# A fused conditional layer and top-1 expert FFN: x gathered by itself, b2 spread by TensorE, the condition sum as one contraction, low halves of x's second half on GpSimd

## The chip, the core and the metric

The kernel runs on one core of a Trainium2 chip. The core has TensorE (PE, matrix products into PSUM), VectorE (DVE), ScalarE (ACT), GpSimd (POOL) and SyncE (SP), which issues DMAs; ScalarE and GpSimd issue DMAs too. The metric is the device time of one execution in microseconds (us), lower is better.

## The reference

2048 tokens of 256 values pass a linear layer whose weights depend on the batch entry, then a feed-forward network with one expert of eight per token, and are added to the input.

```python
# x (2, 1024, 256), cond_8 (2, 8), weight (8, 256, 256), mask (256, 256), bias (256)
masked_w = weight * mask[None, :, :]
w_bot = jnp.einsum('bg,got->bot', y, masked_w)
xf = jnp.einsum('bnt,bot->bno', x, w_bot) + bias        # the conditioned rows
logits = xf @ gate_w.T + gate_b
top1 = jnp.argmax(logits, axis=-1)
for e in range(8):
    h = jax.nn.relu(xf @ w1[e].T + b1[e])               # 256 -> 1024
    y = h @ w2[e].T + b2[e]                             # 1024 -> 256
    out = out + jnp.where((top1 == e)[:, None], y, 0)
return x + out
```

## The kernel before

Products that carry the result are made of float16 pairs: a value is split into a high half (a rounded copy by ScalarE) and a low half (the remainder, by VectorE), and TensorE adds high x high, high x low and low x high. The tokens are sorted by expert into slot tiles of 128 tokens of one expert; this input has 21 such tiles, the first five of expert 0.

**Head.** SP loads y, the eight condition weights in four DMAs of 0.5 MB, the mask, and the transposed x in two halves of 1 MB, then expert 0's four weight chunks and b2, copied to every partition (1 MB). VectorE forms the weighted sum for batch entry 0 in eight steps (lines 603 and 605), TensorE the one for entry 1 with diagonal matrices of y that ScalarE writes (lines 459, 864). Both are multiplied by the mask. `fold_gate` (line 812) multiplies the gate into the sum, `gate_logits` (line 841) gives the logits from x in float32, `turn_w` (line 804) transposes the sum, `w_t_out` and `w_t_low` (lines 469, 621) split it. `x_high(q)` and `x_low(q)` (lines 465, 616) split quarter q of x. `rows(t)` (line 828) makes the conditioned rows of 128 tokens in six matmuls, ScalarE writes them to `xf` (line 503), and SP stores them in five DMAs to the left half of `both_rows` in DRAM (line 347). ScalarE has x copied to its right half by two DMAs of 1 MB (`x_store`, line 485).

**Routing.** VectorE takes the argmax in five steps (lines 661 to 665); TensorE waits for it (`oh_ready`) after three row groups and ranks the tokens; VectorE computes each token's slot, TensorE turns that into `tok_of_slot` (line 894). Each VectorE step waits for the one before (`then`). VectorE then derives a plan for each tile (lines 707 to 726): its expert, and `goal`, how many of the 14 late w2 chunks are split by that tile. It is three per two tiles (`usual_goal`) or two per expert begun, whichever is more.

**Tile loop.** GpSimd gathers the rows of a tile from `both_rows`, 2 KB per token (line 423), eight tiles ahead (`RING`), and scatters the results (line 430). For tile i TensorE transposes the gathered rows of tile i + 1 (`turn_x`, line 916), does layer 1 of tile i (line 928) and layer 2 of tile i - 1 (line 944). ScalarE, in this order: `x_hi(i + 1)`, `w1_high(i + 1)` when its expert is new (two chunks, line 523), the w2 chunks due (`split_chunks`, `high_late`, line 513), `seed_h(i + 1)` (b1 into PSUM, line 543), `h_hi(i)` (line 560), `seed_y(i)` (b2 into PSUM, line 552). VectorE does the low halves in the same order and adds x to the result (`y_out`, line 768). Each engine runs its own list in order.

**Weights.** Each expert has four chunks of 0.5 MB, in the order w1, w2, w1, w2. SP issues them, counts them in `landed` once they have arrived (`confirm`, line 341) and keeps three in flight from expert 2 on. `high_late(m)` waits until 2(m + 2) + 2 chunks have landed. Expert 1's chunks follow the last row store; the last two wait for gathers 0 and 1, expert 2's first for gather 2.

TensorE also does products of ones that nobody reads (`keep_clock_up`, line 855): ten at the start and 24 after the routing. Six more prime the PSUM banks (line 902).

## Time and profile before

| | us |
|---|---|
| median of 3 runs | 173.21 |
| lowest, highest | 172.95, 176.34 |
| the profiled execution | 172.72 |
| its span, first to last instruction | 170.9 |
| TensorE busy | 156.6 |
| VectorE busy | 112.2 |
| ScalarE busy | 106.7 |
| GpSimd busy | 60.1 |

All times in the rows below are of the profiled execution and count from the start of its span; 1.8 us of the time lie outside the span. Busy times are sums over stages with different limits, and TensorE's include the unread products.

### The profile page before, as it was taken

What the parts mean: (1) busy time and instruction counts of PE and PEld (TensorE: products, weight loads), DVE (VectorE), ACT (ScalarE), POOL (GpSimd) and SP (SyncE); (2) the same over time, 40 slices, a digit from 0 to 9 for tenths busy, and PEclk for the clock granted to TensorE, in tenths of its full rate; (3) what the DMA queues carried; (4) which work ended last, traced back from release to release, by engine and by line L of the source; (5) the groups of instructions that cost most, each with busy time, mean ns of one, the idle gap of its engine ahead of it and who ended that gap; (6) DMA issues with size and microseconds to landing.
All of it is one profiled execution on the core that took longest, in us unless ns stands there. A gap on an engine that the chain in (4) does not pass through costs nothing.

```text
span 170.9 us, 6123 instructions
## 1 busy us (share of the span) xinstructions
PE 156.6 (92%) x1807; PEld 132.9 (78%) x1807; DVE 112.2 (66%) x217; ACT 106.7 (62%) x192; POOL 60.1 (35%) x59
## 2 busy tenths in 40 slices
PE   5999899994899999799799799999999999999970
PEld 2347588742689999799789799999999998898850
DVE  0396899980957768999999996345872552258300
ACT  3505988103295988999999968466754465566300
POOL 8300000037830255065666466442464201220222
PEclk9999999999999999999999999999999999999998
DMA  3999999949849788999999912322301101000100
GB/s 71 345 410 411 409 400 385 368 110 332 257 135 314 224 300 303 339 314 295 323 300 344 315 63 84 98 84 65 94 33 42 45 23 35 31 10 31 36 19 19
DMA packets 13797, 33.40 MB, mean 195 GB/s; under 512 B 2619, under 2 KB 6843, under 8 KB 13632
## 3 DMA queue, kind: packets, MB, share of 16 engines
q1 hardware_dynamic: 8288, 24.39, 40.8%
q0 software_dynamic: 2688, 6.30, 11.8%
q10 hardware_dynamic: 2784, 2.26, 4.0%
q8 instruction: 17, 0.28, 0.7%
q14 instruction: 20, 0.16, 0.3%
HBM read 30.06 MB, written 6.95 MB: 217 GB/s over the span
## 4 chain that ended last, share of the span: by engine, by line
PE 57%; DMA 18%; issue 9%; ACT 7%; ACTq 3%; DVE 1%; POOL 1%; SPq 1%; DVEq 1%; POOLq 0%
PE psum L944 21%; PE psum L928 19%; DMA wsp<-w_all 14%; PE psum L828 6%; PE psum L864 4%; PE psum L855 3%; DMA rows_in<-both_rows,tok_of_slot 2%; DMA both_rows<-stage 2%; ACT wsp L513 2%; ACT psum L543 2%; PE psum L916 1%; PE psum L841 1%; PE psum L812 1%; ACTq L284 1%; ACT stage L523 1%
## 5 line engine op out<-in xcount | busy, mean ns | idle before, releaser
L944 PE MATMUL psum<-wsp,hT 128*128 x504 | 58.5, 273 | 1.5 <-issue 1.1
L944 PEld LDWEIGHTS psum<-wsp,hT 128*128 128x128 f16 x504 | 48.1, 98 | 7.8 <-issue 2.6
L763 DVE SCALAR_TENSOR_TENSOR hT<-psum,hT 128x512 f16<-128x512 f32 x42 | 27.3, 687 | 22.6 <-ACT hT L560 22.2
L430 POOL DMA_INDIRECT out<-rows_in,tok_of_slot x17 | 19.9, 1170 | 58.7 <-DVE rows_in L768 58.7
L423 POOL DMA_INDIRECT rows_in<-both_rows,tok_of_slot x17 | 23.4, 1376 | 36.1 <-issue 36.1
L543 ACT ACTIVATE psum<-b_col 128x1024 f32 x21 | 21.5, 1022 | 21.3 <-issue 21.3
L928 PE MATMUL psum<-xs,w1s_own 128*128 128x128 f16 x528 | 31.6, 219 | 0.8 <-issue 0.8
L928 PEld LDWEIGHTS psum<-xs,w1s_own 128*128 128x128 f16 x528 | 30.1, 98 | 2.2 <-issue 1.8
L928 PE MATMUL psum<-xs,stage 128*128 128x128 f16 x480 | 28.4, 219 | 2.8 <-ACT psum L543 2.8
L928 PEld LDWEIGHTS psum<-xs,stage 128*128 128x128 f16 x480 | 27.3, 98 | 3.9 <-issue 2.2
L560 ACT ACTIVATE hT<-psum 128x512 f16<-128x512 f32 x42 | 22.9, 588 | 4.2 <-PE psum L928 2.4
L641 DVE SCALAR_TENSOR_TENSOR wsp<-wsp (+1 forms) x16 | 19.2, 1223 | 6.0 <-ACT wsp L513 4.0
L535 ACT ACTIVATE xs<-psum,bias_col 128x128 f16<-128x128 f32 x42 | 13.2, 369 | 12.0 <-PE psum L916 8.7
L754 DVE SCALAR_TENSOR_TENSOR xs<-psum,bias_col,xs 128x128 f16<-128x128 f32 x42 | 12.7, 346 | 7.4 <-issue 4.7
L513 ACT ACTIVATE wsp<-wsp x14 | 14.9, 1064 | 3.4 <-SPq L341 2.5
L650 DVE SCALAR_TENSOR_TENSOR w1s_own<-wsp,w1s_own 128x1024 f16<-128x1024 f16 (+1 forms) x10 | 11.9, 1223 | 2.3 <-ACT w1s_own L523 2.0
L855 PE MATMUL psum<-ones_h 128*128 128x512 bf16 x38 | 10.8, 445 | 1.9 <-POOL ones L398 1.9
L828 PE MATMUL psum<-stage,wsp 128*128 128x256 f16 x96 | 10.8, 273 | 0.7 <-issue 0.7
L768 DVE SCALAR_TENSOR_TENSOR rows_in<-psum,rows_in 128x256 f32<-128x256 f32 x17 | 7.1, 418 | 5.8 <-PE psum L944 5.8
L828 PEld LDWEIGHTS psum<-stage,wsp 128*128 128x128 f16 x96 | 9.3, 98 | 1.9 <-issue 0.9
L855 PEld LDWEIGHTS psum<-ones_h 128*128 128x128 bf16 x38 | 4.1, 110 | 7.2 <-issue 2.2
L430 POOL DMA_INDIRECT out<-stage,tok_of_slot x4 | 5.4, 1353 | 12.0 <-DVE stage L768 12.0
(113 smaller groups left out, 138.9 us busy)
## 6 DMA issues: line engine op xcount, KB each, us to landing
wsp<-w_all SPq DMA_DIRECT2D x32, 512.0 KB
wsp<-cond_w SPq DMA_DIRECT2D x4, 512.0 KB, 6.8
wsp<-x_t SPq DMA_DIRECT2D x2, 1024.0 KB, 10.7
both_rows<-x_rows ACTq DMA_DIRECT2D x2, 1024.0 KB, 14.8
b_all<-b SPq DMA_DIRECT2D x1, 1024.0 KB, 18.2
both_rows<-stage SPq DMA_DIRECT2D x1, 768.0 KB, 7.3
both_rows<-stage SPq DMA_DIRECT2D x1, 512.0 KB, 6.1
both_rows<-stage SPq DMA_DIRECT2D x1, 384.0 KB, 4.9
```

What stands on the lines that cost most here:

```text
L423: g.indirect_dma_start(slot(i % RING), None, both_rows, token(i), bounds_check=TOK - 1, oob_is_err=False).then_inc(x_in[i % RING], 16)
L430: g.indirect_dma_start(out, token(i), res(i % RING), None, bounds_check=TOK - 1, oob_is_err=False).then_inc(stored[i % RING], 16)
L513: a.mul(hi_of(m + EARLY), raw_w2(m + EARLY), WSCALE).then_inc(hi_ready, 1)
L535: last = a.activation(xs[:, b, 0, k * P:(k + 1) * P], ps_xT[b][:, k * P:(k + 1) * P], ACT.Identity, bias=bias_col[:, k:k + 1])
L543: a.mul(psum[:, 1 + 2 * b:3 + 2 * b, :].rearrange("p q (c n) -> p (q c) n", n=P), b1_col[:, bass.ds(e * KH, KH)].unsqueeze(2).to_broadcast ...
L560: a.activation(hT[:, b, 0, q * HALF:(q + 1) * HALF], ps_h[b][q], ACT.Relu).then_inc(hhi_ready, 1)
L641: v.scalar_tensor_tensor(lo_of(n), raw_w2(n), WSCALE, hi_of(n), ALU.mult, ALU.subtract).then_inc(lo_late, 1)
L763: v.scalar_tensor_tensor(hT[:, b, 1, q * HALF:(q + 1) * HALF], ps_h[b][q], 0.0, hT[:, b, 0, q * HALF:(q + 1) * HALF], ALU.max, ALU.subtrac ...
L828: last = t_.matmul(ps_rows[t % 4], x16[:, xp, k, t * P:(t + 1) * P], w_t[:, b, wp, k * D:(k + 1) * D], start=(k + xp + wp == 0), stop=(k = ...
L855: t_.matmul(psum[:, 6, :], ones_h[:, :], ones_h[:, :].unsqueeze(1).to_broadcast([P, 4, P]), start=True, stop=True)
L928: last = t_.matmul(o, w1s[b][:, w:w + P], xs[:, b, xp, k * P:(k + 1) * P], start=False, stop=(c % 4 == 3 and k == KD - 1 and wp == 1), ski ...
L944: last = t_.matmul(ps_y[b], hT[:, b, hp, c * P:(c + 1) * P], w, start=False, stop=(c == KH - 1 and w is low), skip_group_check=True)
```

## The change

- **Condition sum.** The weights come in four DMAs of 0.5 MB laid out with (16 output rows, 8 conditions) on the 128 partitions. One matrix `y_block`, built by ScalarE from `own_o` (GpSimd) and y, contracts the eight conditions for both batch entries at once on TensorE: 4 x 4 matmuls of 256 columns, each on a strip of 32 columns. The result holds both entries, 16 output rows each, on a strip. VectorE multiplies it by the mask, which is loaded doubled (0.5 MB), in four parts; `fold_gate` and `turn_w` go over the four parts in turn, ahead of the logits. The gate bias is formed in the same layout (16 matmuls of one column). Four unread products stand after each of the first three parts.
- **Small inputs** come in one DMA from ScalarE's queue; the mask and b2 follow there.
- **b2** is loaded once (8 KB) and spread by TensorE (ones times b2, four matmuls of 512 columns in float32) and four ScalarE copies. Two banks are primed in place of six, 16 unread products follow in place of 24.
- **Gathers.** `x_store` goes. A tile's conditioned rows are gathered from `xf_rows` (1 KB per token), and its rows of x by a gather of its own from the input, which `y_out` alone waits for.
- **SP's order.** Expert 0's chunks wait for the first half of x. Two of expert 1's chunks are issued ahead of the row stores and two right behind them. Expert 2's first loads wait for gather 0 in place of gather 2.
- **Low halves.** GpSimd forms `x_low(2)` and `x_low(3)`; VectorE's `w_t_low(1)` and first `w1_low` move; ScalarE does both `w_t_out` ahead of `x_high(0)`, and the first `early_w1_high` after row group 1. The argmax is waited for after four row groups.
- **Goals.** A tile's goal is two w2 chunks for each earlier tile that kept its expert, or two per expert begun, whichever is more. `split_chunks` moves to the end of ScalarE's and VectorE's work on a tile.

```diff
...
-        RANKS_AFTER = 3
-        HIGH_AFTER = (2, 6, 10)
+        RANKS_AFTER = 4
+        HIGH_AFTER = (1, 4, 7, 10)
...
-            sp.dma_start(mask, cond_mask).then_inc(ld_mask, 16)
+            for n in range(OQ):
+                sp.dma_start(condw[:, n, :], cond_w[n]).then_inc(ld_cw[n], 16)
...
+                sp.dma_start(xf_rows[t * P:end * P, :].rearrange("(t p) d -> p t d", p=P),
                              xf[:, t:end, :]).then_inc(rows_stored[n], 16)
...
+            sp.wait_ge(ld_x[0], 16)
             for q in range(CPE):
                 load_chunk(0, q)
-            sp.dma_start(b2_all[:, :, :], b2.partition_broadcast(P)).then_inc(ld_b2, 16)
             for q in range(CPE):
                 confirm(q, 1)
+            for q in range(CPL):
+                load_chunk(1, q)
             for n in range(len(STORES)):
                 store_rows(n)
+            for q in range(CPL, CPE):
+                load_chunk(1, q)
             sp.wait_ge(rows_ps, TT)
-            for n in range(len(STORES)):
-                sp.wait_ge(rows_stored[n], 16)
-            load_chunk(1, 0)
-            load_chunk(1, 1)
             sp.wait_ge(x_in[0], 16)
-            load_chunk(1, 2)
-            sp.wait_ge(x_in[1], 16)
-            load_chunk(1, 3)
             for q in range(CPE):
                 confirm(q, LOADED // CPE)
...
-            sp.wait_ge(x_in[2], 16)
-            sp.wait_ge(wbot0_ready, 1)
-            sp.wait_ge(wbot1_ready, 1)
+            sp.wait_ge(wbot_ready, OQ)
             for q in range(IN_FLIGHT):
                 load_chunk(LOADED // CPE, q)
...
+            for q in (2, 3):
+                pool.wait_ge(x16_hi_ready, q + 1)
+                g.tensor_tensor(x16[:, 1, :, quarter(q)], xT[:, :, quarter(q)], x16[:, 0, :, quarter(q)],
+                                ALU.subtract).then_inc(x16_lo_ready[q], 1)
...
             def gather(i):
                 if i >= RING:
+                    pool.wait_ge(xT_ps, i - RING + 1)
+                g.indirect_dma_start(xg(i % RING), None, xf_rows, token(i),
+                                     bounds_check=TOK - 1, oob_is_err=False).then_inc(x_in[i % RING], 16)
+            def gather_res(i):
+                if i >= RING:
                     pool.wait_ge(stored[i % RING], 16 * (i // RING))
-                g.indirect_dma_start(slot(i % RING), None, both_rows, token(i),
-                                     bounds_check=TOK - 1, oob_is_err=False).then_inc(x_in[i % RING], 16)
+                g.indirect_dma_start(res(i % RING), None, x_rows, token(i),
+                                     bounds_check=TOK - 1, oob_is_err=False).then_inc(res_in[i % RING], 16)
...
-            pool.wait_ge(x_stored, 32)
-            for i in range(RING):
+            for i in range(FIRST):
                 gather(i)
+            for i in range(FIRST, RING):
+                gather_res(i - FIRST)
+                gather(i)
+            for i in range(RING - FIRST, RING):
+                gather_res(i)
...
+                    if_used(pool, used, i + RING - 1, lambda: gather_res(i + RING - 1))
                     if_used(pool, used, i + RING - 1, lambda: gather(i + RING - 1))
...
+            act.dma_start(small[:, :], small_t).then_inc(ld_small, 16)
+            act.dma_start(b2_all[0:1, :, :].rearrange("p e n -> p (e n)"), b2.rearrange("e n -> (e n)").unsqueeze(0)).then_inc(ld_b2, 16)
+            act.dma_start(mask, cond_mask.rearrange("p (a n) -> p a n", a=OQ)).then_inc(ld_mask, 16)
...
+            act.wait_ge(ld_small, 16)
+            act.wait_ge(own_o_ready, 1)
+            for b in range(B):
+                a.mul(y_block[:, b * ON:(b + 1) * ON], own_o[:, :], y_col[:, b:b + 1]).then_inc(y_block_ready, 1)
...
-                act.wait_ge(wT_ps, b + 1)
-                a.mul(w_t[:, b, 0, :], ps_wT[b], WSCALE).then_inc(wT_ready, 1)
+                act.wait_ge(wT_ps, 1)
+                a.mul(w_t[:, b, 0, :].rearrange("p (k a n) -> p k a n", k=KD, n=ON), ps_wT_of[b], WSCALE).then_inc(wT_ready, 1)
...
-            x_store(0)
+            w_t_out(0)
+            w_t_out(1)
             x_high(0)
             x_high(1)
-            x_store(1)
             act.wait_ge(logit_bias_ready, 1)
             act.wait_ge(logits_t_ps, 1)
             a.activation(logits_t[:, 0:XC], ps_logits_t[0], ACT.Identity, bias=logit_bias[:, 0:1]).then_inc(logits_t_ready, 1)
             x_high(2)
-            w_t_out(0)
             x_high(3)
-            w_t_out(1)
-            early_w1_high(0)
...
-                if t == HIGH_AFTER[0]:
-                    early_w1_high(1)
+                if t in HIGH_AFTER[:CPL]:
+                    early_w1_high(HIGH_AFTER.index(t))
                 elif t in HIGH_AFTER:
-                    early_w2_high(HIGH_AFTER.index(t) - 1)
+                    early_w2_high(HIGH_AFTER.index(t) - CPL)
...
+            b2_flat = b2_all[:, :, :].rearrange("p e n -> p (e n)").rearrange("p (a n) -> p a n", n=512)
+            act.wait_ge(b2_ps, 1)
+            for n in range(E * D // 512):
+                a.copy(b2_flat[:, n, :], psum[:, 1 + n, :]).then_inc(b2_ready, 1)
...
                 if_used(act, used, i + 1, lambda: w1_high(i + 1, 1 - b, plan.next_expert, plan.next_expert - plan.expert))
-                if_used(act, used, i + 1, lambda: split_chunks(act, high_late, plan.goal, plan.next_goal))
                 next_plan = following_plan(act, i, plan)
                 if_used(act, used, i + 1, lambda: seed_h(i + 1, 1 - b, plan.next_expert))
                 if_used(act, used, i, lambda: h_hi(i, b))
                 if_used(act, used, i, lambda: seed_y(i, b, plan.expert))
+                if_used(act, used, i + 1, lambda: split_chunks(act, high_late, plan.goal, plan.next_goal))
...
-            v.tensor_tensor(wbot[:, 1, :, :].rearrange("p k n -> p (k n)"), ps_wbot1, mask, ALU.mult).then_inc(wbot1_ready, 1)
+            for n in range(OQ):
+                dve.wait_ge(cond_ps, n + 1)
+                v.tensor_tensor(wbot[:, n, :], ps_cond[n], mask[:, n, :], ALU.mult).then_inc(wbot_ready, 1)
...
+                dve.wait_ge(wT_ready, B)
+                v.scalar_tensor_tensor(w_t[:, b, 1, :].rearrange("p (k a n) -> p k a n", k=KD, n=ON), ps_wT_of[b], WSCALE,
+                                       w_t[:, b, 0, :].rearrange("p (k a n) -> p k a n", k=KD, n=ON),
                                        ALU.mult, ALU.subtract).then_inc(wT_lo_ready, 1)
...
+            dve.wait_ge(gate_ps, 1)
+            v.tensor_copy(gate_w[:, :, :, :].rearrange("p k b n -> p k (b n)"), ps_gate_both).then_inc(gate_w_ready, 1)
+            w_t_low(0)
+            w_t_low(1)
             x_low(0)
             dve.wait_ge(logit_bias_ready, 1)
             dve.wait_ge(logits_t_ps, 2)
             v.tensor_scalar(logits_t[:, XC:2 * XC], ps_logits_t[1], logit_bias[:, 0:1], None,
                             ALU.add).then_inc(logits_t_ready, 1)
             x_low(1)
-            w_t_low(0)
...
-            x_low(2)
-            w_t_low(1)
...
-            x_low(3)
...
-            w1_low(0, 0, 0, 0)
...
-            then(v.tensor_scalar(goal_f[:, 0, :], tile_e[:, :], float(CPL), None, ALU.mult))
-            then(v.tensor_tensor(goal_f[:, 0, :], goal_f[:, 0, :], usual_goal[:, :], ALU.max))
-            then(v.tensor_scalar(goal_f[:, 1, :], goal_f[:, 0, :], float(W2_CHUNKS - EARLY), 0.0, ALU.min, ALU.max))
+            then(v.tensor_tensor(stays[:, 2:NT], tile_e[:, 2:NT], tile_e[:, 1:NT - 1], ALU.is_equal))
+            then(v.tensor_tensor_scan(goal_f[:, 0, :], ones[:, 0:NT], stays[:, :], 0.0, ALU.mult, ALU.add))
+            then(v.tensor_tensor(goal_f[:, 0, :], goal_f[:, 0, :], tile_e[:, :], ALU.max))
+            then(v.tensor_scalar(goal_f[:, 1, :], goal_f[:, 0, :], float(CPL), float(W2_CHUNKS - EARLY), ALU.mult, ALU.min))
...
+            w1_low(0, 0, 0, 0)
...
+                dve.wait_ge(res_in[r], 16 * (i // RING + 1))
...
                 if_used(dve, used, i + 1, lambda: w1_new(i + 1, 1 - b, plan.next_expert, plan.next_expert - plan.expert, plan.next_same))
-                if_used(dve, used, i + 1, lambda: split_chunks(dve, low_late, plan.goal, plan.next_goal))
                 next_plan = following_plan(dve, i, plan)
                 if_used(dve, used, i, lambda: h_lo(i, b, plan.goal))
+                if_used(dve, used, i + 1, lambda: split_chunks(dve, low_late, plan.goal, plan.next_goal))
...
+            def fold_gate(n):
+                for k in range(KD):
+                    last = t_.matmul(ps_gate[k], wbot[:, n, k * P:(k + 1) * P], gate_x[:, n, :],
+                                     start=(n == 0), stop=(n == OQ - 1))
+                if n == OQ - 1:
+                    last.then_inc(gate_ps, 1)
+            def turn_w(n):
+                for k in range(KD):
+                    last = t_.transpose(ps_wT[k][:, n * P:(n + 1) * P], wbot[:, n, k * P:(k + 1) * P], ident[:, :])
+                if n == OQ - 1:
+                    last.then_inc(wT_ps, 1)
...
+            pe.wait_ge(y_block_ready, B)
+            for n in range(OQ):
+                pe.wait_ge(ld_cw[n], 16)
+                for j in range(CG):
+                    last = t_.matmul(ps_cond[n][j * EP:(j + 1) * EP, :], y_block[:, :], condw[:, n, j * D:(j + 1) * D],
+                                     start=True, stop=True)
+                last.then_inc(cond_ps, 1)
+                if n < OQ - 1:
+                    keep_clock_up(CLOCK_GAP)
+                if n == 0:
+                    for q in range(OQ):
+                        for j in range(CG):
+                            last = t_.matmul(ps_gate_bias[j * EP:(j + 1) * EP, :], gate_x[:, q, 0:EP], bias_x[:, q:q + 1],
+                                             start=(q == 0), stop=(q == OQ - 1))
+                    last.then_inc(gate_bias_ps, 1)
+            pe.wait_ge(logit_bias_ready, 1)
+            for n in range(OQ):
+                pe.wait_ge(wbot_ready, n + 1)
+                fold_gate(n)
+                turn_w(n)
             gate_logits(0)
             gate_logits(1)
-            turn_w(0)
+            rows(0)
             pe.wait_ge(logits_t_ready, 2)
             turn_logits(0)
             turn_logits(1).then_inc(logits_ps, 1)
-            turn_w(1)
-            for t in range(RANKS_AFTER):
+            for t in range(1, RANKS_AFTER):
                 rows(t)
...
                     t_.matmul(psum[:, 3, 0:D], ones_h[:, :], ones_h[:, :].unsqueeze(1).to_broadcast([P, 2, P]),
                               start=True, stop=True)
             pe.wait_ge(rows_ready, TT)
-            for bank in range(1, 7):
+            pe.wait_ge(ld_b2, 16)
+            pe.wait_ge(consts, N_CONST)
+            for n in range(E * D // 512):
+                last = t_.matmul(psum[:, 1 + n, :], ones[0:1, :], b2_all[0:1, 2 * n:2 * n + 2, :].rearrange("p e n -> p (e n)"),
+                                 start=True, stop=True)
+            last.then_inc(b2_ps, 1)
+            for bank in range(5, 7):
                 last = t_.matmul(psum[:, bank, :], ones_h[:, :], ones_h[:, :].unsqueeze(1).to_broadcast([P, 4, P]),
                                  start=True, stop=True)
...
-            keep_clock_up(24)
+            keep_clock_up(16, 6)
             pe.wait_ge(experts_known, 1)
...
```

## Rows read from the trace of the kernel before

**Rows 1.** The page's chain that ended last, by line.

```profile
PE psum L944 21%; PE psum L928 19%; DMA wsp<-w_all 14%; PE psum L828 6%; PE psum L864 4%; PE psum L855 3%; DMA rows_in<-both_rows,tok_of_slot 2%; DMA both_rows<-stage 2%; ACT wsp L513 2%; ACT psum L543 2%; PE psum L916 1%; PE psum L841 1%; PE psum L812 1%; ACTq L284 1%; ACT stage L523 1%
```

**Rows 2.** The chain in order of time: start us, us, what.

```profile
22.34 8.53 PE psum L828 x78
31.30 4.14 DMA both_rows<-stage
...
49.93 4.73 DMA wsp<-w_all
...
62.83 5.49 DMA wsp<-w_all
...
100.88 2.68 PE psum L928 x48
103.55 2.62 PE psum L944 x24
```

**Rows 3.** Busy time by window: engines, then granted clock, DMA share, GB/s.

```profile
6.00:14.00 8.00, 7.97 (x24) 3.67 (x23) 6.85 (x10) 0.73 (x4) 0.00 (x0) 1.00 1.03 407
60.00:98.00 38.00, 35.33 (x474) 32.79 (x472) 35.20 (x52) 36.20 (x58) 20.20 (x12) 1.00 0.94 315
```

**Rows 4.** Timeline, TensorE, first layer of tiles 0, 5 and 9.

```profile
43.61 2.62 PE L928 MATMUL psum<-xs,w1s_own 128*128 128x128 f16 x40 [0.33 <-issue]
...
70.80 2.84 PE L928 MATMUL psum<-xs,stage 128*128 128x128 f16 x48 [0.89 <-ACT psum L543]
...
95.19 2.84 PE L928 MATMUL psum<-xs,stage 128*128 128x128 f16 x48 [0.85 <-ACT psum L543]
```

**Rows 5.** Timeline, ScalarE, splits of weights.

```profile
65.17 2.00 ACT L523 ACTIVATE stage<-wsp 128x1024 f16 x2
...
68.68 1.06 ACT L513 ACTIVATE wsp<-wsp  x1 [0.56 <-SPq L341]
```

**Rows 6.** Line 327, the condition weights' DMAs: issues, and us to landing.

```profile
L327 SPq DMA_DIRECT2D wsp<-cond_w x4: 408/432/723, 1.3 to 2.7; - x4
...
DMA to landing us min/median/max: 4.9/6.8/8.1
```

**Rows 7.** Timeline, TensorE, head.

```profile
1.88 4.42 PE L855 MATMUL psum<-ones_h 128*128 128x512 bf16 x10 [1.88 <-POOL ones L398]
...
6.33 7.23 PE L864 MATMUL psum<-wsp,hT 128*128 128x512 f32 x16
...
13.76 1.95 PE L812 MATMUL psum<-gate,stage 128*128 128x32 f32 x16
...
15.64 2.01 PE L841 MATMUL psum<-wsp,gate_w 128*32 128x256 f32 x32
```

**Rows 8.** Timeline, ScalarE and VectorE, head.

```profile
14.74 1.04 ACT L465 CAST wsp<-wsp 128x1024 f16<-128x1024 f32 x1 [0.48 <-issue]
...
18.27 0.60 ACT L469 ACTIVATE stage<-psum 128x512 f16<-128x512 f32 x1
...
19.92 0.28 DVE L661 TENSOR_REDUCE best<-psum 128x16 f32<-128x128 f32 x1
...
21.21 0.71 DVE L665 TENSOR_TENSOR oh<-e_less,first 128x128 bf16<-128x128 f32 x1
```

**Rows 9.** Timeline, TensorE, from the routing to the first transpose.

```profile
34.20 5.34 PE L855 MATMUL psum<-ones_h 128*128 128x512 bf16 x24
41.80 0.41 PE L916 MATMUL psum<-ident,rows_in 128*128 128x128 f32 x2 [2.26 <-DMA rows_in<-both_rows,tok_of_slot]
```

**Rows 10.** Timeline, GpSimd, and one VectorE instruction beside it.

```profile
2.93 2.65 POOL L414 MEMSET rows_in<- 128x3072 f32 x1
...
36.59 1.18 POOL L423 DMA_INDIRECT rows_in<-both_rows,tok_of_slot  x1 [31.01 <-issue]
...
76.03 1.22 DVE L641 SCALAR_TENSOR_TENSOR wsp<-wsp  x1
76.16 2.01 POOL L423 DMA_INDIRECT rows_in<-both_rows,tok_of_slot  x1 [0.30 <-issue]
```

182 lines of the change are left out of this document (75 added, 107 removed).

## The prediction

> **What bounds the kernel now.** I read the page's chain by line first, then the chain in order of time, then the windows, then the timelines of the stretches that change. The chain is 40% TensorE's two expert layers (lines 944 and 928) and 14% a wait for expert weights [rows 1]. In order of time it has three parts [rows 2]. The head, up to the first expert tile at 43.6 us [rows 4], runs through the condition sum, the logits, the 16 matmul groups of the conditioned rows (line 828, last piece ending 30.87), the last store of those rows (4.14 us) and the gather. Then comes a stretch bound by weights: the chain's loads land at 54.7 and 68.3. From 95.19 TensorE alone sets the pace, 2.68 + 2.62 and 0.22 for two transposes, 5.52 us per tile.
>
> DMA moves 407 GB/s in the head and 315 at a share of 0.94 between 60 and 98 [rows 3]. From the first tile (43.61) to the tenth (95.19) TensorE takes 51.6 us, where tile 0 (4.06 before the next starts) and eight at 5.52 would be 48.2 [rows 4]. The missing 3.4 us are stalls of about 1 us ahead of tiles 5, 7 and 9. The first follows ScalarE's split that could start only at 68.68, when expert 3's last chunk had landed [rows 2, 5]; the other two come of ScalarE, which in each of these tiles splits 1.5 w2 chunks beside 2 w1 chunks, at 1.0 to 1.06 us each [rows 5]. The later 71.5 us are TensorE's and the change doesn't touch them.
>
> **Condition sum and gate.** Removed: 8 VectorE steps, 16 matmul records of 512 columns (lines 603 to 607, 864), ScalarE's 8 y_diag. Added on TensorE, which is free of the warm-up at 6.3 [rows 7]: 16 matmuls of 256 columns on 32-column strips, 32 records. Line 841 does 32 such records in 2.01, so 2.0 in all. 12 clock dummies at 0.22 (5.34/24, rows 9): 2.7. The gate bias in 32 one-column records: between nothing and the 0.125 of line 812's records; nearest in weights are line 841's at 0.063, and one column streams less, so I take 0.04: 1.3. Sum 12.3. The last cond_w chunk landed 8.1 after its issue at 2.7, at 10.8 [rows 6]. The doubled mask puts 0.26 MB more beside it (0.6 us at 407 GB/s, rows 3) and the small loads, merged into one, give some back: about 11.3, so TensorE decides. Fold and turn are 24 records at 0.125 [rows 7]: 3.0, so the transposed weights stand at 15.3 and gate_w at 15.6. The gate logits still end with x, whose bytes ahead change by +0.26 MB: 17.5, against 17.65 [rows 7]. So the faster contraction buys nothing: x sets this point.
>
> **The order behind it.** ScalarE now does both w_t halves (0.60 each) ahead of x_high, so that x_high(0), 1.04, begins at 16.6 and not 14.74 [rows 8]. VectorE: w_t low twice (I take 0.7 each, 512 elements from PSUM beside ScalarE's 0.60) to 18.0, x_low(0) (1.22, as line 641 on 1024 elements, rows 10) to 19.2, logits_t to 19.7, x_low(1) to 20.9; argmax then takes the 2.0 between 19.92 and 21.92 [rows 8] and ends at 22.9, a microsecond later than before. TensorE puts row groups 0 to 3 ahead of it, idles 0.3, and does the other 12 at 0.67 (8.53/13 with its gaps): end 31.35, against 30.87. x_low(2) and (3), and the w1 low half, leave VectorE's chain behind the argmax, 3 times 1.2. That chain then ends about with the row groups, so routing is not later than before.
>
> **GpSimd's two subtractions.** GpSimd has no such row. From below, its 3072-element memset took 2.65 [rows 10], so 1024 elements take 0.9; from above, if each of the three operands went at that rate, 2.6. They may start at about 20 and are wanted at 26.3 (group 8) and 29 (group 12): hidden either way for TensorE. What they cost VectorE is the first rival.
>
> **Stores, gathers, b2.** x_store (2.1 MB) and the broadcast b2 (1.05 MB) leave the head's DMA, which was saturated until the last store; 1.05 MB of expert 1 moves in at about 22. The last store should take 3.2 in place of 4.14 [rows 2], bounds 2.8 and 4.1. So gather 0 is issued at 36.1 (36.59 before, rows 10), is half as large and meets no 1 MB load issued just ahead of it: 3.5 in place of 5.2, landed at 39.6 against 41.8 [rows 9]. It is what SP waits for before expert 2's first load: 39.6 in place of 49.93 [rows 2], the largest shift of the change. GpSimd issues 16 gathers in place of 8, at 1.3 each, until 57, then three DMAs per tile (up to 1.7 + 2.0 + 2.0 + 0.9 = 6.6 us beside VectorE's splits, rows 10) against 5.5. It falls behind by some 10 us over tiles 0 to 9, covered by the seven tiles (38 us) that a gather runs ahead. Without the cover each tile would cost 1.1.
> TensorE pays for b2: 4 matmuls of 512 columns, two f32 records each, as line 864's 16 between 6.33 and 13.56, of which those without a wait took 0.43 [rows 7]: 3.4; four priming matmuls and 8 dummies fewer, 2.7 less. From 31.35: token matmuls 2.2, b2 3.4, priming 0.4, 16 dummies 3.6, register loads 0.3: first transpose at 41.2 against 41.80 [rows 9], so tile 0 at 43.0 against 43.61. ScalarE's four b2 copies (0.6 each) end at 39.3, ahead of that. TensorE, not the gather, is now last here.
>
> **Split goals.** Tiles 0 to 4 are expert 0 (ScalarE splits w1 anew first ahead of tile 5, rows 5). The new goals put two w2 chunks in each of tiles 0 to 3 and none in tiles 4 to 7, so the stalls ahead of tiles 7 and 9 go. But by the end of iteration 3 the 20th chunk must have landed (expert 4's last), where the old goals wanted the 16th. In the trace the 16th landed at 68.3, 18.4 after expert 2's first issue [rows 2], and a chunk took 1.95 (13.6 us for 7). From 39.6 that gives 39.6 + 18.4 + 4 x 1.95 = 65.8. Behind it on ScalarE and VectorE: the split 1.06, x_hi 0.6, two w1 highs 2.0, the last w1 low 1.2 and 0.5 of order: tile 5 at 71.2, against 70.80. TensorE could have come at 69.1 (43.0 + 4.06 + 4 x 5.52), so the weights stay the bound there. Then four tiles at 5.52: tile 9 at 93.3, against 95.19.
>
> **The sum.** -1.9 us: +0.4 at tile 5 and -2.3 between tiles 5 and 9. The profiled execution was 172.72 with a span of 170.9, so the new span is 169.0 and that execution 170.8; the median of the runs is 0.5 higher, hence 173.2 - 1.9 = 171.3. Its own range is 169.8 to 172.8: the store and gather bounds 1.3, the gate bias 1, the chunk rate 1.
>
> **Rivals.**
> *GpSimd holds VectorE.* Gather DMAs take 1.18 on GpSimd alone and 2.01 when VectorE's two-input split runs beside them [rows 10]: in these rows the two wait for one another, and GpSimd loses as the later one. If the earlier one wins, x_low(2) on GpSimd starts when x_low(1) ends (20.9) and holds the two-input step of line 663 from 21.5 until it ends; x_low(3) then holds line 665. At 2.6 per subtraction: 2.0 + 2.3 = 4.3 on the argmax; at 1.3: 1.6; at 0.9: 0.9. TensorE waits for the argmax before group 4, so all of it passes on: 175.6, 172.9 or 172.2. From 1.4 us per subtraction on, the kernel ends slower than before. Against it: no VectorE row of the trace grows beside GpSimd. The Trainium skill (SBUF — State Buffer, Who interferes with whom) says a VectorE instruction with two SBUF inputs and a GpSimd one that reads SBUF exclude each other for the whole instruction, the first issued winning. The skill's GPSIMD Engine Reference (Engine selection) puts two-input elementwise work at about twice VectorE's time; by the two pages the sum would be 175.2.
> *The weights come in time.* Alone, 0.52 MB at 315/0.94 GB/s is 1.57 us. At 1.6 per chunk the 20th lands at 62 and TensorE sets tile 5: 69.1, tile 9 at 91.2, -4.0: 169.2. For it: 3.1 MB less DMA ahead. Against: 16 gathers fall in the same stretch.
> *The clock falls.* Every window grants 1.00, yet the first ten dummies took 0.44 each and later ones 0.22 [rows 7, 9]. TensorE idles at about 18 us and, with the first rival, 4 us more. If groups 4 to 15 ran at 1.2 GHz in place of 2.4, they would cost up to 8 us: 177 to 179. Against: an idle of 2.26 at 39.5 [rows 9] cost nothing that shows.
> *No effect* (each gain hidden behind TensorE's dummies and the weights): 173.
>
> **Chances.** Main case 0.36, GpSimd holds VectorE 0.32, weights in time 0.20, clock 0.06, no effect 0.06. The range takes the first three: 168.6 to 175.6. Faster by over 2% (about what a measurement of this kernel can tell from no change), below 169.7: 0.26, the third case and the edge of the first. Slower, above 176.7: 0.07. Within: 0.67.
>
> **What would show it.** Right: TensorE's first tile near 43, expert 2's first load issued near 40, a wait of 2 us ahead of tile 5 ended by a weight chunk, none ahead of tiles 7 and 9. Lock: line 663's or 665's successor two microseconds long, or a gap ahead of row group 4. Weights in time: no wait at tile 5. Wrong head: the last row group ending before 30 or after 33.

## The result, and the profile after

The change makes the kernel slower. Six runs of the changed kernel took 174.19 to 177.38 us, median 176.06; the kernel before on the same chip had a median of 173.1. The ratio is 1.013, with a 95% interval of 1.008 to 1.018. The forecast was 171.3 with a range of 168.6 to 175.6. Here and below, a ratio compares executions in the chip's faster state only while a median takes them all, so where the two disagree the ratio counts.

The profiled execution of the changed kernel took 174.19 us, the shortest of its runs, with a span of 172.5. That is 1.6 us more span than the 170.9 of before. It is read here against the profiled execution of before (172.72), and the forecast stands against the same scale.

That execution shows 1.5 us of the loss and the medians show 3. Four of the other five took 1.6 to 2.6 us longer than it, and their mean granted clocks were 0.966 to 0.962 against its 0.975, the longer the time the lower the clock. Worked out from these numbers, that is 3 to 4.5 us more at the lower clock level, an estimate, which costs TensorE about half of that. Where in the kernel it fell isn't seen, as only one execution was profiled. The fifth took 177.38 at 0.977, which this doesn't explain.

The chain of the changed kernel in order of time (start us, us, what) is the outline. Compare [rows 2].

```profile
20.40 1.58 DVE hT L671
22.00 0.30 DVE first L672
22.32 2.18 DVE oh L673
24.56 0.29 PE psum L896
24.95 9.07 PE psum L832 x72
34.05 0.39 ACT stage L522
34.46 2.89 DMA xf_rows<-stage
37.58 0.60 issue
38.41 3.15 DMA rows_in<-xf_rows,tok_of_slot
...
42.71 7.75 DMA wsp<-w_all
```

All five steps of the argmax are on the chain, three of them in these lines; in the kernel before none was. The row groups follow late and long, 9.07 us for 12, and everything behind them is late: the last store begins at 34.46 (31.30 in [rows 2]), gather 0 is issued at 38.41 (36.59 in [rows 10]). The store itself did get cheaper, 2.89 us against 4.14, and expert 2's first load moved forward from 49.93 to 42.71.

The timelines of VectorE and GpSimd between 18 and 25 us show why the argmax is long (start us, us, engine, line, operation, output<-input, shapes):

```profile
19.08 4.87 POOL L433 TENSOR_TENSOR wsp<-wsp 128x1024 f16<-128x1024 f32 x2 [13.14 <-ACT wsp L494]
20.07 0.29 DVE L670 TENSOR_TENSOR hT<-psum,best 128x128 f32<-128x128 f32 x1
20.40 1.57 DVE L671 TENSOR_TENSOR hT<-hT,e_less 128x128 f32<-128x128 f32 x1
...
22.32 2.17 DVE L673 TENSOR_TENSOR oh<-e_less,first 128x128 bf16<-128x128 f32 x1
```

Line 671 is line 663 of before:

```profile
20.56 0.29 DVE L663 TENSOR_TENSOR hT<-hT,e_less 128x128 f32<-128x128 f32 x1
```

Line 673 is line 665, 0.71 in [rows 8]. They grew by 1.28 and 1.46 us, 2.74 together, beside the two subtractions of GpSimd, which took 2.74 and 2.17 us. Lines 670 and 672 lie beside GpSimd as well and didn't grow; the first has one of its inputs in PSUM, the second is a reduction with one input in SBUF. GpSimd was held too: its first subtraction began while VectorE was still at `x_low(1)` (18.62 to 19.84) and took 2.74, where each takes 2.13 in e2. The argmax began 0.2 us earlier than before (19.75, 19.92 in [rows 8]) and ended 2.6 us later, at 24.49.

TensorE's timeline carries that on, and a second thing with it:

```profile
24.56 0.29 PE L896 MATMUL psum<-oh,before 128*128 128x128 bf16 x1 [2.93 <-DVE oh L673]
24.74 9.27 PE L832 MATMUL psum<-stage,wsp 128*128 128x256 f16 x72
35.97 3.70 PE L913 MATMUL psum<-b_all,ones 1*128 1x512 f32 x8
40.04 5.30 PE L859 MATMUL psum<-ones_h 128*128 128x512 bf16 x16
...
46.97 2.84 PE L943 MATMUL psum<-xs,w1s_own 128*128 128x128 f16 x48 [0.33 <-issue]
73.90 2.85 PE L943 MATMUL psum<-xs,stage 128*128 128x128 f16 x48 [0.81 <-DVE stage L658]
95.99 2.84 PE L943 MATMUL psum<-xs,stage 128*128 128x128 f16 x48
```

The last three lines answer to [rows 4]: tiles 0, 5 and 9 begin at 46.97, 73.90 and 95.99, where they began at 43.61, 70.80 and 95.19. So the head lost 3.4 us, and 2.6 of them came back between tiles 0 and 9 (49.02 us in place of 51.58). The 16 unread products of line 859 took 0.33 us each, where 24 took 0.22 each in [rows 9]. The windows say what that is (window, busy time of PE, PEld, DVE, ACT and POOL, granted TensorE clock, DMA share, GB/s):

```profile
22.00:24.00 2.00, 0.00 (x0) 0.00 (x0) 1.96 (x2) 0.23 (x1) 1.95 (x1) 0.97 0.19 51
24.00:26.00 2.00, 1.44 (x8) 1.10 (x9) 1.44 (x5) 0.00 (x0) 0.00 (x0) 0.50 0.91 252
26.00:28.00 2.00, 2.00 (x15) 1.54 (x13) 1.73 (x10) 1.61 (x3) 0.00 (x0) 0.68 0.54 221
...
38.00:40.00 2.00, 2.00 (x6) 0.58 (x5) 1.71 (x10) 0.25 (x1) 1.28 (x2) 1.00 0.92 346
40.00:42.00 2.00, 2.00 (x8) 0.79 (x7) 1.83 (x2) 1.81 (x4) 1.70 (x2) 0.73 0.29 98
42.00:44.00 2.00, 2.00 (x6) 0.73 (x5) 0.00 (x0) 1.03 (x1) 1.70 (x2) 0.50 0.70 178
44.00:46.00 2.00, 2.00 (x11) 0.97 (x9) 0.00 (x0) 0.40 (x2) 1.39 (x3) 0.91 0.89 293
```

The granted clock falls twice to 0.50, which is 1.2 GHz. The first time is at the end of the idle of 2.93 us that the argmax leaves (0.97 in 22 to 24), and it stays down while TensorE does the first row groups. The second time TensorE hadn't been idle at all: it is busy for all of 36 to 44, but from 35.97 to 39.6 with matmuls of one row ("1\*128", the b2 spread).

Three questions went to the chip: what the hold on VectorE costs, what makes the clock fall the second time, and why so little of an earlier start reaches the end.

### The profile page after: what moved, and what is told of

It reads as the page before. It is cut to its first block, busy times and chain, and to the rows that moved or that the text cites. A ratio compares the mean times of both kernels' runs of the same rounds, so it can differ in the third digit from the quotient of the medians.

```text
span 172.5 us, 6267 instructions
## 1 busy us (share of the span) xinstructions
PE 157.7 (91%) x1859; PEld 132.6 (77%) x1859; DVE 108.2 (63%) x209; ACT 106.4 (62%) x190; POOL 83.5 (48%) x85
## 4 chain that ended last, share of the span: by engine, by line
PE 65%; DMA 17%; DVE 6%; issue 5%; ACT 2%; POOL 1%; SPq 1%; POOLq 1%; ACTq 0%; DVEq 0%
PE psum L943 25%; PE psum L959 25%; DMA wsp<-w_all 14%; PE psum L832 5%; PE psum L859 4%; DMA rows_in<-xf_rows,tok_of_slot 2%; PE psum L931 2%; DMA xf_rows<-stage 2%; PE psum L868 1%; DVE wsp L627 1%; DVE oh L673 1%; PE psum L809 1%; DVE hT L671 1%; SPq L350 1%; DVE stage L658 1%
## 5 line engine op out<-in xcount | busy, mean ns | idle before, releaser
L455 POOL DMA_INDIRECT out<-rows_in,tok_of_slot x17 | 18.1, 1066 | 30.6 <-issue 16.0
L442 POOL DMA_INDIRECT rows_in<-xf_rows,tok_of_slot x17 | 20.7, 1215 | 19.4 <-issue 19.0
L562 ACT ACTIVATE psum<-small 128x1024 f32 x21 | 21.5, 1023 | 7.3 <-issue 6.3
L448 POOL DMA_INDIRECT rows_in<-x_rows,tok_of_slot x17 | 20.4, 1200 | 10.5 <-DMA out<-rows_in,tok_of_slot 4.6
L554 ACT ACTIVATE xs<-psum,small 128x128 f16<-128x128 f32 x42 | 13.0, 363 | 17.8 <-PE psum L931 17.8
L760 DVE SCALAR_TENSOR_TENSOR xs<-psum,small,xs 128x128 f16<-128x128 f32 x42 | 12.7, 344 | 8.1 <-ACT xs L554 7.9
L532 ACT ACTIVATE wsp<-wsp x14 | 14.2, 1054 | 2.9 <-SPq L355 1.5
L859 PE MATMUL psum<-ones_h 128*128 128x512 bf16 x42 | 13.9, 488 | 1.9 <-POOL ones L405 1.9
L832 PE MATMUL psum<-stage,wsp 128*128 128x256 f16 x96 | 12.2, 291 | 0.3 <-DVE wsp L627 0.3
L832 PEld LDWEIGHTS psum<-stage,wsp 128*128 128x128 f16 x96 | 10.0, 105 | 2.4 <-issue 0.8
```

The source lines that it names most:

```text
L442: g.indirect_dma_start(xg(i % RING), None, xf_rows, token(i), bounds_check=TOK - 1, oob_is_err=False).then_inc(x_in[i % RING], 16)
L448: g.indirect_dma_start(res(i % RING), None, x_rows, token(i), bounds_check=TOK - 1, oob_is_err=False).then_inc(res_in[i % RING], 16)
L455: g.indirect_dma_start(out, token(i), res(i % RING), None, bounds_check=TOK - 1, oob_is_err=False).then_inc(stored[i % RING], 16)
L532: a.mul(hi_of(m + EARLY), raw_w2(m + EARLY), WSCALE).then_inc(hi_ready, 1)
L562: a.mul(psum[:, 1 + 2 * b:3 + 2 * b, :].rearrange("p q (c n) -> p (q c) n", n=P), b1_col[:, bass.ds(e * KH, KH)].unsqueeze(2).to_broadcast ...
L832: last = t_.matmul(ps_rows[t % 4], x16[:, xp, k, t * P:(t + 1) * P], w_t[:, b, wp, k * D:(k + 1) * D], start=(k + xp + wp == 0), stop=(k = ...
```

## The experiments

| kernel | median us | ratio to the kernel before (95%) | tile 0, 5, 9 of the profiled execution |
|---|---|---|---|
| before | 173.1 to 174.5 | 1 | 43.61, 70.80, 95.19 |
| changed | 176.06 | 1.013 (1.008 to 1.018) | 46.97, 73.90, 95.99 |
| e1_dve_low | 172.56 | 0.995 (0.991 to 1.000) | 45.06, 72.67, 94.75 |
| e2_low_after_argmax | 172.00 | 0.990 (0.986 to 0.994) | 44.88, 71.27, 93.36 |
| e3_b2_by_dma | 177.80 | 1.030 (1.013 to 1.047) | 44.91, 74.35, 97.77 |
| e4_dve_low_b2_by_dma | 176.85 | 1.024 (1.011 to 1.038) | 41.82, 74.17, 98.14 |
| e5_clock_kept_up | 173.36 | 0.998 (0.993 to 1.003) | 47.33, 73.88, 95.96 |
| e6_gpsimd_low_on_before | 177.32 | 1.016 (1.004 to 1.028) | 45.65, 73.41, 100.19 |
| e7_goals_between | 172.88 | 0.997 (0.994 to 1.001) | 45.97, 71.93, 95.33 |
| e8_four_in_flight | 173.18 | 0.995 (0.990 to 1.000) | 44.73, 71.13, 93.21 |
| e9_b2_all_rows | 172.37 | 0.982 (0.974 to 0.990) | 42.70, 71.69, 95.17 |
| e10_b2_rows_four | 170.44 | 0.977 (0.971 to 0.983) | 42.64, 69.04, 91.38 |
| e11_six_unread | 169.19 | 0.972 (0.966 to 0.978) | 41.88, 70.06, 93.78 |
| e12_old_goals | 175.03 | 1.000 (0.995 to 1.004) | 45.98, 71.94, 96.37 |

The kernel before was run with each group; its median was 174.2 beside e1 to e8 and 174.5 beside e9 to e12, and the groups ran on other chips than the two kernels above, so the ratios are the measure across groups. Those of e6 and e9 rest on two executions each.

### e1: the subtractions back on VectorE

```diff
-            for q in (2, 3):
-                pool.wait_ge(x16_hi_ready, q + 1)
-                g.tensor_tensor(x16[:, 1, :, quarter(q)], xT[:, :, quarter(q)], x16[:, 0, :, quarter(q)],
-                                ALU.subtract).then_inc(x16_lo_ready[q], 1)
...
                             ALU.is_equal).then_inc(oh_ready, 1)
+            x_low(2)
...
             then(v.tensor_tensor(offs[:, 2, :], offs[:, 0, :], offs[:, 1, :], ALU.subtract))
+            x_low(3)
```

> The changed kernel with one part undone: x_low(2) and x_low(3) are VectorE's again, at their old places. Port theory (GpSimd's two subtractions hold VectorE's two-input steps of the argmax): the step of line 671 falls from 1.57 to 0.29 us and that of line 673 from 2.17 to 0.71, the argmax ends near 21.8 in place of 24.5, TensorE's wait ahead of row group 4 shrinks from 2.9 to under 0.5, its clock stays granted in full there, and the last row group ends near 31 in place of 34. Since a microsecond of the old saving on VectorE comes back as two subtractions of 1.2 us, the tile loop starts 2.5 to 3.5 us earlier and the time is 3 us less (about 173). Rival, weights: if the arrival of expert 4's last chunk alone sets tile 5 and does not move with the head, the time is under 1 us less.

Measured: 172.56 us, ratio 0.995, where the changed kernel had 1.013. VectorE's timeline:

```profile
20.59 0.29 DVE L667 TENSOR_TENSOR hT<-hT,e_less 128x128 f32<-128x128 f32 x1
...
21.24 0.71 DVE L669 TENSOR_TENSOR oh<-e_less,first 128x128 bf16<-128x128 f32 x1
```

Both steps have their old length, the argmax ends at 21.9, the clock stays at 1.00 from 20 to 28, and the row groups take 8.02 us again and end at 30.15 in place of 34.0. So the hold and the first fall of the clock belong to GpSimd's work. Of these 3.9 us only 1.9 reach tile 0 (46.97 to 45.06), and 1.2 reach tiles 5 and 9. The b2 matmuls begin 3.6 us earlier (32.42, 35.97 in the changed kernel), but the clock falls while they still run, so that they take 5.01 us in place of 3.70; and at tile 5 TensorE waits 1.44 us for the weights. The tile loop was expected 2.5 to 3.5 us earlier, so the hold was right and its worth was not.

### e2: the same subtractions on GpSimd, but behind the argmax

```diff
+            pool.wait_ge(oh_ready, 1)
             for q in (2, 3):
                 pool.wait_ge(x16_hi_ready, q + 1)
```

> The changed kernel with GpSimd's two subtractions kept, but begun only when the argmax is done. Port theory: the argmax steps are short again (0.29 and 0.71), since nothing on GpSimd runs beside them; the subtractions (2.4 us each) then run beside VectorE's ranking and end near 27, ahead of row group 12 but about at row group 8, and may stretch a few of the small two-input steps by 1 to 2 us, which have 0.7 us of room before TensorE's token products. Time 2 to 3.5 us less than the changed kernel. Rival (work moved to GpSimd costs by its length, not by its overlap): no gain, since TensorE waits for the low halves instead of for the argmax.

Measured: 172.00 us, ratio 0.990. One line of order turns a kernel that is 1.3% slower than before into one that is 1% faster. The hold didn't disappear, it moved:

```profile
22.29 4.22 POOL L434 TENSOR_TENSOR wsp<-wsp 128x1024 f16<-128x1024 f32 x2 [16.34 <-DVE oh L674]
23.23 1.21 DVE L682 TENSOR_SCALAR padded_i<-count 128x8 int32<-128x8 f32 x1
24.48 2.06 DVE L683 TENSOR_SCALAR padded_i<-padded_i 128x8 int32<-128x8 int32 x1
```

These are tiny steps of eight elements with a single SBUF input, 0.17 us each in the changed kernel and in e1. Beside GpSimd, whose two subtractions took 2.13 each, they took 1.21 and 2.06. TensorE has 12 row groups to do meanwhile, and most of it is covered: the row groups end at 30.4, the b2 matmuls begin at 33.88, 1.5 us later than in e1 and 2.1 earlier than in the changed kernel. Tile 0 came 2.1 us earlier than in the changed kernel (44.88), and tiles 5 and 9 2.6 us.

### e3 and e4: b2 by DMA again

The b2 spread by TensorE is replaced by the broadcast DMA of 1 MB, six primed banks and 24 unread products of the kernel before; e4 has e1's edit as well.

```diff
             for q in range(CPE):
                 load_chunk(0, q)
+            sp.dma_start(b2_all[:, :, :], b2.partition_broadcast(P)).then_inc(ld_b2, 16)
...
-            for n in range(E * D // 512):
-                last = t_.matmul(psum[:, 1 + n, :], ones[0:1, :], b2_all[0:1, 2 * n:2 * n + 2, :].rearrange("p e n -> p (e n)"),
-                                 start=True, stop=True)
-            last.then_inc(b2_ps, 1)
-            for bank in range(5, 7):
+            for bank in range(1, 7):
...
-            keep_clock_up(16, 6)
+            keep_clock_up(24, 6)
```

> The changed kernel with one part undone: b2 is copied to all partitions by a DMA of 1 MB behind expert 0's chunks, the four f32 products with one row and ScalarE's four copies go, six banks are primed and 24 unread products follow as before. GpSimd keeps the subtractions. Clock theory: the eight records that use a single row of the array let the clock fall to half from 40.5 to 44.5 us; without them it stays full, TensorE is free at 36 + 1.3 + 5.3 = 42.7 in place of 45.2, and tile 0 starts near 44.5 in place of 47.0. Expert 4's last chunk still lands at 67.7 or up to 1 us later for the added 1 MB, so tile 5 stays near 73.9: the time is 0 to 1 us less in the profiled execution. If TensorE's start set the end instead, it would be 2.5 us less.

> Both parts undone together: VectorE has all four low halves and b2 comes by DMA. If the two cost what the trace of the changed kernel says, the head is 3 us shorter by the first and TensorE is free 2.5 us earlier by the second: tile 0 near 41.5, expert 2's first load near 38.5 to 39.5, expert 4's last chunk at 64.5 to 65.5, tile 5 near 71, tile 9 near 93. Time about 4 us less than the changed kernel, 172 or 1 us below the kernel before. If the weights' arrival sets the loop, this run beats the one with VectorE's low halves alone by less than 1 us.

Measured: 177.80 and 176.85 us, both slower than before, where up to 1 us less than the changed kernel (e3) and about 172 us (e4) were expected. Without the one-row matmuls the clock stayed at 1.00 from 36 to 44 in both: the second fall goes with them. The first is still there: TensorE waits 3.38 us for the argmax, the clock stands at 0.50 from 26 to 28, and the row groups take 9.69 us. In e3 part of the hold changed its place, as GpSimd began 0.31 us ahead of `x_low(1)` (18.51 and 18.82):

```profile
18.82 2.91 DVE L623 TENSOR_TENSOR wsp<-wsp 128x1024 f16<-128x1024 f32 x1
```

VectorE's subtraction took 2.91 in place of 1.22, GpSimd's kept its 2.13, and the argmax began late, at 21.65; of its two steps only the first was held after that (1.57 and 0.69). In the changed kernel `x_low(1)` had begun first and GpSimd's was the longer one. So whichever of the two began first held the other.

And e4 has the earliest first tile of all kernels, 41.82, which is 5.2 us ahead of the changed kernel, and still loses. ScalarE's timeline of e4, and then TensorE's, show where it goes:

```profile
68.28 1.06 ACT L528 ACTIVATE wsp<-wsp  x1 [3.37 <-SPq L355]
```

```profile
74.17 4.74 PE L931 MATMUL psum<-xs,stage 128*128 128x128 f16 x48 [5.66 <-DVE stage L650]
...
81.59 2.84 PE L931 MATMUL psum<-xs,w1s_own 128*128 128x128 f16 x48
```

The eighth late split waits 3.37 us for the 20th weight chunk, which is there at 67.9, no earlier than in the changed kernel (67.7), where 64.5 to 65.5 was expected. TensorE idles 5.66 us ahead of tile 5, and layer 1 of tile 5 then takes 4.74 us where every other took 2.84, because the clock had fallen in the idle. So the earlier start of TensorE was lost twice, once as idle and once as 1.9 us of slow clock. Part of e4's loss is the broadcast's own: e1 has the same head without it, and there SP sees gather 0 landed at 38.4 and the 20th chunk at 66.4, against 40.1 and 67.9 here. How much of the ratio each part holds isn't shown; e9 has an early start without the broadcast.

### e5: the clock kept up through the wait for the argmax

Twelve unread products fill TensorE's wait; GpSimd's subtractions stay where the change has them.

```diff
+            pe.wait_ge(wT_lo_ready, B)
+            keep_clock_up(12, 1)
             pe.wait_ge(oh_ready, 1)
```

> The changed kernel with GpSimd's subtractions where they are, and 12 more unread products of 512 columns on TensorE ahead of its wait for the argmax (12 x 0.22 = 2.7 us, about the length of the wait). It parts the two costs of the overlap. Port theory: the steps of lines 671 and 673 stay long (about 1.6 and 2.2 us). Clock theory: the granted clock stays at 1.00 through 22 to 28 us, where it fell to 0.50 and 0.68, and row groups 4 to 15 take 8.0 us in place of 9.3, so the head is 1.2 us shorter and the time about 1.2 us less (if the weights follow the head). If the clock fell for another reason than the idle time, it falls again and nothing is gained.

Measured: 173.36 us, ratio 0.998, where the changed kernel had 1.013. Two windows, and then TensorE's timeline:

```profile
22.00:24.00 2.00, 2.00 (x11) 0.82 (x9) 1.94 (x2) 0.28 (x2) 1.98 (x1) 1.00 0.41 106
24.00:26.00 2.00, 1.68 (x16) 1.30 (x15) 1.52 (x6) 0.44 (x2) 0.00 (x0) 1.00 0.88 287
```

```profile
24.71 8.02 PE L832 MATMUL psum<-stage,wsp 128*128 128x256 f16 x72
```

The argmax is as late as in the changed kernel (lines 671 and 673 took 1.58 and 2.18), but the row groups take 8.02 us in place of 9.27 and end 1.3 us earlier. So the first fall follows from the idle and costs 1.3 us. The gain at the row groups doesn't show at tile 0 of this profiled execution (47.33): there the second fall came sooner and was longer, three windows at 0.50 from 38 to 44, and the b2 matmuls took 4.35 and the 16 products 5.91. Tiles 5 and 9 begin where the changed kernel has them (73.88, 95.96), and the 0.8 us less of span lies behind them. So the 1.3 us are shown at the row groups and not at the end, and what the ratio's gain consists of stays open.

### e6: the subtractions on GpSimd, in the kernel before

```diff
+            for q in (2, 3):
+                pool.wait_ge(x16_hi_ready, q + 1)
+                g.tensor_tensor(x16[:, 1, :, quarter(q)], xT[:, :, quarter(q)], x16[:, 0, :, quarter(q)],
+                                ALU.subtract).then_inc(x16_lo_ready[q], 1)
...
-            x_low(2)
...
-            x_low(3)
```

> The kernel before with one part of the change alone: GpSimd forms x_low(2) and x_low(3). Port theory: it starts as soon as x_high(2) is done (18.3) or x_low(1) ends (19.4) and runs for about 4.9 us beside the argmax, so the two-input steps of lines 663 and 665 grow by 1 to 2 us each and the argmax ends near 24.5 in place of 21.9; the row groups end 2.5 to 3.5 us later for it and for the clock. VectorE gets 2.4 us back behind the argmax, which does not help TensorE. Time 2 to 3 us more than the kernel before. Rival (the moved work helps, as it unloads VectorE, and other parts cost): 0 to 1 us less.

Measured: ratio 1.016, from two executions of 174.97 and 177.01 us, with an interval of 1.004 to 1.028. This one edit makes the kernel before slower, by about as much as the whole change did. VectorE's timeline:

```profile
20.88 0.98 DVE L668 TENSOR_TENSOR hT<-hT,e_less 128x128 f32<-128x128 f32 x1
...
22.22 2.17 DVE L670 TENSOR_TENSOR oh<-e_less,first 128x128 bf16<-128x128 f32 x1
```

The same two steps grew, from 0.29 and 0.71, without any other part of the change, and the row groups ended 2.4 us later. The clock did not fall there, behind a wait of 1.90 us. It fell at the first tile, behind a wait of 2.06 for gather 0, and layer 1 of tile 0 took 4.13 us in place of 2.84. The profiled execution took 177.63 and overstates the edit: its stalls ahead of tiles 7 and 9 are 2.23 and 1.89 us, where before has 0.92 and 0.85, and why they grew isn't shown. If the medians are taken at their word, the other parts together were worth about nothing; the next runs take that apart.

### e7 and e12: the goals

In e7 and e12 and in the runs behind them e2 is the base. e7 lets a tile's goal rise only as fast as the old one did; e12 has the old goals.

```diff
-            then(v.tensor_tensor_scan(goal_f[:, 0, :], ones[:, 0:NT], stays[:, :], 0.0, ALU.mult, ALU.add))
-            then(v.tensor_tensor(goal_f[:, 0, :], goal_f[:, 0, :], tile_e[:, :], ALU.max))
-            then(v.tensor_scalar(goal_f[:, 1, :], goal_f[:, 0, :], float(CPL), float(W2_CHUNKS - EARLY), ALU.mult, ALU.min))
+            then(v.tensor_tensor_scan(kept[:, :], ones[:, 0:NT], stays[:, :], 0.0, ALU.mult, ALU.add))
+            then(v.scalar_tensor_tensor(kept[:, :], kept[:, :], float(CPL), usual_goal[:, :], ALU.mult, ALU.min))
+            then(v.scalar_tensor_tensor(goal_f[:, 0, :], tile_e[:, :], float(CPL), kept[:, :], ALU.mult, ALU.max))
+            then(v.tensor_scalar(goal_f[:, 1, :], goal_f[:, 0, :], float(W2_CHUNKS - EARLY), 0.0, ALU.min, ALU.max))
```

In e12 the second of the added lines is a plain copy of `usual_goal`.

> The kernel with GpSimd's subtractions after the argmax, and other goals: two w2 chunks per tile that kept its expert, but no more than the old three per two tiles, and at least two per expert. So iterations 0 to 7 split 0, 1, 2, 1, 2, 1, 1 and 0 late chunks, and tile 5 needs the 16th landed chunk and not the 20th. Weights theory: the wait ahead of tile 5 that a weight chunk ends goes or shrinks to the 0.3 us of ScalarE's order; tile 5 starts near 70.5 or earlier with tile 0 near 44.9. Rival: ScalarE is the bound again in tiles 5 to 8 (4.9 us of its own and up to 1.1 of a split against 5.5), so tiles 6 and 7 wait 0.5 us each and the sum is as before. Between -1.0 and +0.5 us against the kernel it is made from (172.0).

> Edit: as e2_low_after_argmax, with the goals of the kernel before (three w2 chunks per two tiles, or two per expert begun); the place of the splits at the end of a tile's work stays. Theory: the stalls of about 1 us ahead of tiles 7 and 9 come from the goals (1.5 w2 chunks beside 2 w1 chunks), so they come back: tile 9 at 93.36 + 1.1 + 1.0 = 95.5, while tile 5 may begin up to 0.2 earlier, as only the 16th chunk is needed there: time 174.0, 2.0 more than e2. Rival (the stalls had gone because the splits moved behind h_hi): no stalls ahead of tiles 7 and 9, tile 9 within 0.3 of 93.36, time 172.0.

Measured: ratios 0.997 and 1.000, against 0.990 for the base; e7 with 172.88 us against 172.00 lies outside the -1.0 to +0.5 that was expected. In both profiled executions tile 0 begins 1.1 us later than in e2, as the clock had fallen sooner (0.63 and 0.50 in 36 to 38, 1.00 in e2), so the goals are read from the distances between tiles. In e7 tile 5 begins with no wait at all, 25.96 us behind tile 0, but 1.3 us are lost ahead of tile 6, and tile 9 is 49.4 us behind tile 0 where e2 has 48.5. TensorE's timeline of e12 has the same stall and another:

```profile
71.94 2.84 PE L948 MATMUL psum<-xs,stage 128*128 128x128 f16 x48
78.77 2.85 PE L948 MATMUL psum<-xs,w1s_own 128*128 128x128 f16 x48 [1.15 <-DVE w1s_own L662]
84.30 2.84 PE L948 MATMUL psum<-xs,stage 128*128 128x128 f16 x48
90.81 2.85 PE L948 MATMUL psum<-xs,w1s_own 128*128 128x128 f16 x48 [0.83 <-DVE w1s_own L662]
```

Tiles 5 to 6 and 7 to 8 are 6.83 and 6.51 us apart where the rest is 5.5: 2.3 us of stalls. From tile 0 to tile 9 it is 50.4 us, 1.9 more than e2's 48.5 and 2.1 expected. The size is right and the place isn't: the stalls came ahead of tiles 6 and 8, not 7 and 9 as expected. A likely reason, not tested, is that the splits now stand at the end of a tile's work and delay the next but one. The rival (the stalls had gone because the splits moved) falls. The new goals are worth about 1.9 us; the prediction had 2.3 between tiles 5 and 9.

### e8: four chunks in flight

```diff
-IN_FLIGHT = 3
+IN_FLIGHT = 4
```

> The kernel with GpSimd's subtractions after the argmax and four weight chunks in flight in place of three. If a chunk's 1.95 us is the DMA engines' limit beside the gathers, it stays, and with it the time within 0.3 us (or it grows, as the gathers come later). If the round trip of issue and landing holds it back, it falls to 1.6 us, expert 4's last chunk lands 3 us earlier, no weight chunk ends a wait ahead of tile 5, and the time is 0.5 to 1 us less than with three.

Measured: ratio 0.995, no better than e2. The windows from 58 to 66, first e2, then e8:

```profile
58.00:66.00 8.00, 8.00 (x103) 7.42 (x102) 6.20 (x11) 6.63 (x11) 3.36 (x4) 1.00 0.89 295
```

```profile
58.00:66.00 8.00, 8.00 (x106) 7.57 (x105) 6.20 (x11) 6.63 (x11) 3.21 (x4) 1.00 1.00 361
```

The loads did get faster, 361 GB/s against 295, so three in flight didn't fill the DMA engines. TensorE just wasn't waiting for them in e2 (0.15 us ahead of tile 5): tile 5 came 26.40 us behind tile 0, and tile 0 hadn't moved. Its ten executions lie in two clusters: four at 171.13 to 171.66 us with mean granted clocks of 0.980 to 0.985, six at 173.13 to 173.62 with 0.970 to 0.975. So the clusters go with the clock; the profiled execution (171.66) is of the lower one, and where the clock fell in the other isn't seen.

### e9: b2 spread over all 128 rows

Base e2. The b2 spread keeps its four float32 matmuls of 512 columns, but they go over 128 rows, 127 of them zero.

```diff
+            g.memset(b2_all[:, :, :], 0.0).then_inc(b2_zero, 1)
...
+            a.copy(first_row[:, :], ident[:, 0:1].to_broadcast([P, P])).then_inc(first_ready, 1)
...
-                last = t_.matmul(psum[:, 1 + n, :], ones[0:1, :], b2_all[0:1, 2 * n:2 * n + 2, :].rearrange("p e n -> p (e n)"),
+                last = t_.matmul(psum[:, 1 + n, :], first_row[:, :], b2_all[:, 2 * n:2 * n + 2, :].rearrange("p e n -> p (e n)"),
```

> Edit: as e2_low_after_argmax, and b2 is spread by the same four float32 matmuls of 512 columns, but over all 128 rows of the array: b2_all is zeroed by GpSimd in the head, b2 lands in its row 0, and the stationary operand is the first column of the identity spread over 128 columns in place of a row of ones. In e2 the granted clock fell to 0.65 and 0.50 in the windows 38:40 and 40:42 right behind these matmuls, the 16 unread products took 5.30 (0.33 each, 0.22 at the full clock), and tile 0 began at 44.88. Theory A (a matmul that fills one row of 128 doesn't count as work for the clock): the granted clock stays at 1.00 from 34 to 46, the 16 products take 3.6, tile 0 begins at 43.2, 1.7 earlier. Theory B (the clock falls for another reason, a gap in front or the float32 form): the clock falls as in e2, products 5.3, tile 0 at 44.9. Time: expert weights limit tile 5 (71.27 in e2, with a wait of 0.15 only). If A, tile 5 can begin at 69.6 by TensorE but the 20th chunk landed at about 66 and the splits behind it give about 70.5: 171.3; if B, 172.0.

Measured: ratio 0.982. The windows of e2, for comparison:

```profile
38.00:40.00 2.00, 2.00 (x8) 0.82 (x7) 1.85 (x2) 1.72 (x4) 1.48 (x2) 0.65 0.32 80
40.00:42.00 2.00, 2.00 (x6) 0.64 (x5) 0.00 (x0) 1.03 (x1) 1.70 (x2) 0.50 0.92 248
```

TensorE's timeline, and then two windows:

```profile
33.52 3.67 PE L921 MATMUL psum<-b_all,first_row 128*128 128x512 f32 x8
...
37.46 3.62 PE L866 MATMUL psum<-ones_h 128*128 128x512 bf16 x16
```

```profile
38.00:40.00 2.00, 2.00 (x11) 0.88 (x9) 1.33 (x2) 1.66 (x4) 1.70 (x2) 1.00 0.16 37
40.00:42.00 2.00, 2.00 (x12) 1.08 (x11) 0.01 (x1) 1.32 (x3) 1.39 (x3) 1.00 0.85 234
```

Theory A holds: the matmuls take the same time (3.67 and 3.70), the granted clock stays at 1.00, the 16 products take 3.62 in place of 5.30, and tile 0 begins at 42.70, 2.2 us ahead of e2. In the matmuls nothing changed but the number of rows. Around them there are a memset of GpSimd (1.79 us at 3.30), a ScalarE copy of 0.29 at 3.15, and b2's load behind the mask, all in the first 6 us. The other kernels agree: in the profiled executions of the seven with one-row matmuls (changed, e1, e2, e5, e7, e8, e12) the clock fell beside or behind them, and of the five without (e3, e4, e9, e10, e11) in none between 34 and 46. At tile 5 the expectation was too good (70.5):

```profile
71.69 4.25 PE L951 MATMUL psum<-xs,stage 128*128 128x128 f16 x48 [2.87 <-DVE stage L665]
...
78.61 2.84 PE L951 MATMUL psum<-xs,w1s_own 128*128 128x128 f16 x48
```

This is e4 again without the broadcast: the 20th chunk is there at 65.5 (64.1 in e2), TensorE waits 2.87 us, the clock falls and layer 1 takes 4.25. The profiled execution took 173.61 at a mean granted clock of 0.985; two of the other three took 170.70 and 171.44 at 0.991 and 1.000, and in the last the clock can't have fallen at tile 5.

### e10: all rows and four in flight

> Edit: as e9_b2_all_rows, and four weight chunks in flight in place of three. In e8, four in flight raised the traffic between 50 and 66 from 339 and 295 GB/s to 370 and 361, without moving tile 5, which TensorE set by then (71.13, tile 0 at 44.73, distance 26.40). If the clock holds through the b2 spread (theory A of e9) both limits are gone together: tile 0 at 43.2, tile 5 at 43.2 + 26.1 = 69.3, tile 9 at 91.4, time 170.2, 1.7% below the kernel before. If the clock falls as before (theory B): tile 0 at 44.7, time as e8, 171.7 to 173.2.

Measured: 170.44 us, ratio 0.977. TensorE's timeline:

```profile
42.64 2.84 PE L951 MATMUL psum<-xs,w1s_own 128*128 128x128 f16 x48 [0.32 <-issue]
...
69.04 2.85 PE L951 MATMUL psum<-xs,stage 128*128 128x128 f16 x48 [0.28 <-DVE stage L665]
...
91.38 2.84 PE L951 MATMUL psum<-xs,stage 128*128 128x128 f16 x48
```

Expected were 43.2, 69.3, 91.4 and 170.2. Four in flight, worth nothing in e8, now turns e9's wait of 2.87 us into 0.28, with the 20th chunk there at 61.8 in place of 65.5, and keeps the clock up through tile 5. In the profiled executions the earlier start and the faster weights pay in full only together. The ratios say less: 0.982 and 0.977 have intervals that overlap (0.974 to 0.990, 0.971 to 0.983).

### e11: six unread products in place of sixteen

> Edit: as e10_b2_rows_four, with 6 unread products after the b2 spread in place of 16 (2.2 us less at the full clock). Theory A (what comes first, the first transpose, waits for TensorE alone): TensorE is free 2.2 us earlier, and tile 0 moves by up to that, to 41.0 to 42.0; it can't begin before gather 0 has landed (41.6 in the profiled execution of the changed kernel, earlier by up to 1 us where the row groups end earlier) plus 1.8, about 42.2. Then tile 5 follows at 68.3 if the weights allow, else it waits for them as in e4_dve_low_b2_by_dma (wait of 2 us and more, the clock falls to 0.5 during tile 5, and the kernel loses 1 to 2 us). Rival: TensorE idles ahead of the first transpose and the granted clock falls there, layer 1 of tile 0 takes 4 to 5 us in place of 2.8. Time 169.3 by the theory, 172 and more by either loss.

Measured: 169.19 us, ratio 0.972 (0.966 to 0.978), the lowest of all, with an interval that overlaps e10's. Tile 0 begins at 41.88, where 42.2 was expected as the bound by gather 0; both first transposes now wait for their gathers, 0.16 and 0.59 us, so the head has no more slack in TensorE. The profiled execution took 171.96, above its own other four (168.87 to 169.77): the 20th chunk was there only at 63.8, tile 5 waited 2.06 us and began at 70.06 where 68.3 was expected, and the clock fell. What tile 5 did in the faster executions isn't seen. Two of them had mean granted clocks of 1.000 and 0.999, against 0.990 of the profiled one, so in these the clock didn't fall there.

## Why the prediction was wrong

**The point that failed: "GpSimd's two subtractions ... hidden either way for TensorE", with "GpSimd holds VectorE" only as a rival.** The price was about right. I gave 0.9 to 2.6 us per subtraction, and it is 2.13 where VectorE doesn't hold it (e2), 2.17 for the second and 2.74 for the first in the changed kernel. What failed is the choice between cases. The rival said that from 1.4 us on the kernel ends slower than before, and gave 175.6 at 2.6 us; the median came at 176.06. That it came so near is partly luck, as the rival's own sum at the measured hold, 171.3 and 2.74, is 174.0, and the rest is the clock, which it didn't have. It had named line 663 and line 665 as the steps that would be held, and those are the ones that grew, by 1.28 and 1.46 us. The hold is 2.74 and not 4.3, as a subtraction ends about 2.1 us and not 2.6 behind the point where it is free to run: the first ended at 21.82, 1.98 us behind the end of x_low(1), the second 2.17 us later. (Two sums of the rival are 0.1 off: 1.3 us per subtraction gives 1.7 and 173.0, and the two pages' price gives 175.3.) e1, e2 and e6 show the cause from both sides.

My argument against it was that "no VectorE row of the trace grows beside GpSimd". No such row could exist there: in the kernel before GpSimd did nothing between 5.58 and 36.59 us [rows 10], so nothing of it lay beside the argmax. Against this stood one row that did show an exclusion, GpSimd's gather of 2.01 us beside a two-input split in place of 1.18 [rows 10], and I read it as a reason for 0.32 only. The Trainium skill (SBUF — State Buffer, Who interferes with whom) says that a VectorE instruction with two SBUF inputs and a GpSimd one that reads SBUF exclude each other for a whole instruction. The trace agrees for lines 671 and 673. The same section names tensor_scalar among the steps with one input that can be held, and says that tensor_reduce never is. The trace agrees with both: e2's lines 682 and 683, TENSOR_SCALAR, were held for 1.04 and 1.89 us, and line 672 of the changed kernel, TENSOR_REDUCE, kept its 0.29.

**The clock.** I gave "the clock falls" 0.06 and argued that an idle of 2.26 us had cost nothing [rows 9]. The idle of 2.93 us did: 0.50 from 24 to 26, and 1.3 us on the row groups (9.27 against 8.02; e5 takes it back). I had put "up to 8 us" there, far too much, as the full clock was back after about 3 us. The second fall was in no case of mine. I priced b2 as 3.4 us of matmuls and 3.6 of unread products; they took 3.70 and 5.30. The unread products were there to keep the clock up, and one-row matmuls ahead of them undid it. e9 shows that rows are the cause.

**The head's sum.** Tile 0 was forecast for 43.0 and began at 46.97. Of the 3.97 us, about 2.65 lie ahead of the end of the last row group (34.0 against 31.35): the argmax ended 1.6 later than forecast, and the clock cost 1.25. The other 1.3 lie between it and tile 0, where the 16 products took 1.5 more than their term (40.04 to 45.18, against 3.6) and b2 0.2, and the token matmuls and the register loads 0.5 less. The steps in front were close: the condition sum on TensorE done at 12.0 (12.3 forecast), the transposed weights at 14.7 (15.3), the logits at 18.07 (17.5) behind a wait of 0.99 us for x. The last is as predicted: x sets this point, and the faster contraction bought nothing. The argmax began at 19.75 where I had 20.9, as the w_t low halves took 0.65 each and ran a microsecond earlier.

**Stores and gathers.** The last store took 2.89 (3.2 forecast), gather 0 3.15 from its issue (3.5). Both are as forecast; the store starts 2.7 us late and the gather 2.3. Expert 2's first load followed gather 0 by design, at 42.71.

**Weights.** Right in its step and wrong in its start. The 20th chunk landed at 67.65, 26.1 us behind gather 0's landing at 41.58; 26.2 were forecast (65.8 less 39.6). Tile 5 came 6.25 us later, 5.4 forecast, with a wait of 0.81 us. So "the weights stay the bound there" was right, and e3, e4 and e9 show it from the other side: with tile 0 at 41.8 to 44.9, tile 5 stays at 71.7 to 74.4. The arrival itself varies: behind the landing of gather 0 the 20th chunk took 25.4 us in e2, 26.6 in e9 and 28.0 in e1, and why isn't shown. What I missed is that this bound makes an earlier start of TensorE worth little, and less still through the clock. "The weights come in time" (0.20) gave 69.1 and 91.2 for tiles 5 and 9 if a chunk came faster; e10, with four in flight, has 69.04 and 91.38.

**Goals.** Right: no stalls ahead of tiles 7 and 9, and 22.09 us from tile 5 to tile 9, 22.1 forecast. e12 gives 1.9 us for it in a run of its own.

**The end.** From tile 9 on TensorE takes the same time, but the profiled execution ends 0.8 us later than that. In the chain GpSimd's last scatter is issued 2.06 us behind TensorE's last matmul in place of 1.25, behind a piece of 0.98 us on GpSimd's queue and 2.82 of issue. It is so in the profiled executions of the changed kernel, e2, e3, e4, e9 and e11, and not in those of before, e1, e5, e6, e7, e8, e10 and e12, nearly the same programs. From the last scatter's end to the end of the span it is 2.0 to 2.4 us in most and 3.1 to 3.8 in e1, e7, e8, e10 and e12. I didn't find what decides either, and both stay open.

## What to carry to other kernels

Before work is given to GpSimd, list which VectorE instructions will run beside it and who waits for them: an instruction can be held for as long as GpSimd's lasts, so the move is free only where VectorE has slack of that length, and one wait that puts it behind the urgent steps (e2) is worth 2.3% here. TensorE's clock has to be counted with every new wait and every new matmul shape: here idle or one-row matmuls ahead of real work made that work 1.2 to 1.7 times as long (9.27 us for 8.02, 4.74 for 2.84). And where a chain of loads runs beside TensorE, an earlier start and faster loads are to be tried together: faster loads alone measured as nothing (e8), and the earlier start alone ran into a wait and a fallen clock (e9), which both together didn't (e10).

## What the runs showed of the hardware

- **GpSimd holds VectorE even for tiny instructions.** TENSOR_SCALAR steps of 8 elements with one SBUF input took 1.21 and 2.06 us in place of 0.17 beside a GpSimd subtraction of 1024 elements (e2). A step with an input in PSUM beside it kept its 0.29 us, and so did a TENSOR_REDUCE (lines 670 and 672 of the changed kernel).
- **The one that begins first holds the other.** GpSimd's subtraction beginning 0.31 us ahead of VectorE's kept its 2.13 us, and VectorE's took 2.91 in place of 1.22 (e3); beginning 0.46 us behind it, GpSimd's took 2.74 (the changed kernel).
- **One-row matmuls don't keep the clock up.** Eight float32 records over one row, TensorE busy all the time, were followed by a granted clock of 0.50; the same records over 128 rows, of equal length (3.67 and 3.70 us), by 1.00 (e2 and e9). In e1 the clock fell while the one-row records still ran, and they took 5.01 us.
- **Idle drops the clock, and when it does varies.** Waits of 2.06, 2.06, 2.87, 2.93, 3.38 and 5.66 us (e6, e11, e9, the changed kernel, e3, e4) were each followed by a fallen clock and cost 1.3 to 1.9 us on the work behind them; one of 2.26 us in the kernel before cost nothing that shows [rows 9], and 1.90 and 2.23 us in e6 neither.
- **Three loads of 0.5 MB in flight didn't fill the DMA engines**: share 0.89 and 295 GB/s, with four 1.00 and 361 (e2 and e8, 58 to 66 us).
- **A two-input subtraction on GpSimd** (128x1024, float32 less float16 to float16) took 2.13 us unhindered (e2), VectorE's takes 1.22.
